# A graph network's softmax stage with attention and message columns interleaved by input feature

## The reference

```python
w_m = (efeat @ W_msg + b_msg).reshape(E, in_f, -1)
w_a = (efeat @ W_attn + b_attn).reshape(E, in_f, -1)
h_src = feat[src][:, :, None]
e1 = w_m * h_src
e2 = w_a * h_src
seg_max = jax.ops.segment_max(e2, dst, num_segments=N)
ex = jnp.exp(e2 - seg_max[dst])
denom = jax.ops.segment_sum(ex, dst, num_segments=N)
attn = ex / denom[dst]
ft = jax.ops.segment_sum(e1 * attn, dst, num_segments=N)
return ft.sum(axis=1)
```

## Time and profile before

| what | value |
|---|---|
| median of three runs | 9786.86 us |
| span of the profiled execution | 9780.2 us (the fastest of the three runs took 9780.59 us) |
| softmax loop | from 3036 to 6483 us of the span |
| one block in the loop | 20.7 us on average |
| DVE operations in the loop | 39 per block, 165 blocks |
| granted TensorE clock in the loop | 1.00 |
| other layers (conv1, conv2, rel, nn) | the rest, 6330 us |

### The profile page before, as it was taken

How to read it: one execution, slowest core, us unless ns; L and a number is a source line. 1 busy time by engine, 2 the same in 40 slices (tenths; PEclk the granted TensorE clock), 3 DMA queues, 4 the chain that set the end, 5 groups by cost and what they waited for, 6 DMA issues and landing times.

```text
span 9780.2 us, 134112 instructions
## 1 busy us (share of the span) xinstructions
PE 7946.4 (81%) x37269; PEld 4276.1 (44%) x37269; DVE 7357.8 (75%) x13651; ACT 3060.5 (31%) x12664; POOL 7256.3 (74%) x5177
## 2 busy tenths in 40 slices
PE   0899996999984777777777777745999995899994
PEld 0466663555541333333333333323655554555552
DVE  2566663454545999999999999987888885688884
ACT  0111111000004777777777777742000000000000
POOL 5677775777767777777777777745888887688887
PEclk6999996999997999999999999977999997899997
DMA  1333332222213777777777777766222221333331
GB/s 32 101 101 106 104 101 52 67 60 68 68 46 91 202 201 200 202 205 201 200 201 203 203 202 200 201 186 190 70 82 69 82 69 47 99 106 99 99 104 48
DMA packets 490722, 1215.28 MB, mean 124 GB/s; under 512 B 236141, under 2 KB 273304, under 8 KB 469836
## 3 DMA queue, kind: packets, MB, share of 16 engines
q1 hardware_dynamic: 242522, 996.22, 31.8%
q0 software_dynamic: 212624, 110.62, 9.1%
q10 hardware_dynamic: 35440, 106.85, 3.3%
HBM read 419.84 MB, written 787.23 MB: 123 GB/s over the span
## 4 chain that ended last, share of the span: by engine, by line
PE 27%; POOL 26%; issue 23%; DVE 19%; DMA 2%; DVEq 1%; SPq 1%; ACT 0%; POOLq 0%; ACTq 0%
POOL arena L559 26%; PE PS L949 21%; DVE arena L1687 5%; DVE arena L1691 4%; PE PS L971 4%; DVE arena L1733 3%; DVE arena L1700 2%; DVE arena L1711 2%; PE PS L932 1%; DVEq L1679 1%; DVE arena L1813 1%; DMA arena<-d_lane 0%; DVE tmp L1815 0%; DVE arena L1422 0%; DVE arena L1721 0%
## 5 line engine op out<-in xcount | busy, mean ns | idle before, releaser
L949 PE MATMUL PS<-arena,TB 125*128 125x500 bf16 (+1 forms) x18711 | 4067.9, 373 | 109.2 <-DVE arena L1390 109.1
L559 POOL DMA_INDIRECT arena<-d_feat,srci x1650 | 2578.1, 1562 | 842.0 <-issue 454.2
L949 PEld LDWEIGHTS PS<-arena,TB 125*128 125x128 bf16 x18711 | 1832.9, 99 | 2013.2 <-issue 174.7
L559 POOL DMA_INDIRECT arena<-d_h,srci x1485 | 1887.5, 1271 | 653.0 <-issue 433.1
L770 ACT ACTIVATE arena<-PS,arena 125x32 f32<-125x32 f32 x10560 | 2012.4, 446 | 302.8 <-PE PS L1068 263.0
L1390 DVE TENSOR_SCALAR arena<-arena,lane 125x2000 bf16<-125x2000 f16 (+2 forms) x1848 | 1228.9, 723 | 348.0 <-PE PS L949 221.9
L1402 DVE SCALAR_TENSOR_TENSOR arena<-arena,lane,PS 128x500 f32<-128x500 f16 x891 | 637.1, 715 | 1120.9 <-PE PS L949 858.5
L559 POOL DMA_INDIRECT arena<-d_rel,irel x858 | 1210.2, 1411 | 307.2 <-issue 261.2
L559 POOL DMA_INDIRECT arena<-d_nn,srci x759 | 1068.6, 1408 | 283.4 <-issue 230.4
L1115 PE MATMUL PS<-arena,ident 125*125 125x512 f32 x1650 | 873.6, 610 | 403.6 <-ACT arena L813 210.1
L1733 DVE SCALAR_TENSOR_TENSOR arena<-arena 125x512 f32<-125x512 f32 x1155 | 859.7, 744 | 20.3
(11 more groups left out here) (274 smaller groups left out, 7172.5 us busy)
## 6 DMA issues: line engine op xcount, KB each, us to landing
d_soft_max<-arena SPq DMA_DIRECT2D x165, 1120.0 KB
d_soft_den<-arena SPq DMA_DIRECT2D x330, 560.0 KB
d_soft_num<-arena SPq DMA_DIRECT2D x330, 560.0 KB
arena<-d_pick SPq DMA_DIRECT2D x66, 843.8 KB
arena<-d_lane SPq DMA_DIRECT2D x66, 843.8 KB
d_x<-arena ACTq DMA_DIRECT2D x165, 241.7 KB
arena<-d_x SPq DMA_DIRECT2D x165, 241.7 KB
d_rel<-arena SPq DMA_DIRECT2D x50, 669.4 KB
```

The costliest lines, as they stand in the source:

```text
L559: gp.indirect_dma_start(out=dst, out_offset=None, in_=table, in_offset=bass.IndirectOffsetOnAxis(ap=index, axis=0)).then_inc(S(sem), 16)
L949: ins = pe.matmul(PS[:, acc_at(L, q):acc_at(L, q) + w], TB[:, part, g * LANES * F:(g + 1) * LANES * F], OH[L][i][:, g, at:at + w], start=g ...
```

## The change

The 512 columns of `W6` are put in another order: for each input feature i, 16 attention columns and then 16 message columns. So everything behind it is interleaved as well: `XS` is parted into `XM` (maxima, 256 numbers per edge) and `XD` (pairs, 512 per edge, i x (attention, message) x 16), and a helper `paired(rows, a)` picks the attention (a = 0) or the message (a = 1) runs of 16 numbers.

With pairs interleaved, one `product` covers a whole group of two edges: 1024 elements, three per block where there were six. ACT's `scaled` reads and writes 32 numbers in one run. `weigh` now works on 2, 4 and 4 edges (three operations, 512, 1024 and 1024 elements, called w0, W2, W6) instead of five times 2. The maxima of n0 to n9, the exponentials, the first subtraction matmul and `weigh` now read or write runs of 16 numbers, 32 apart. The two sum tables become `low` and `high`, the first and the last 256 numbers of a pair row: in each, a piece of a store is 1024 bytes where it was 5120, five times as many pieces for the same bytes. Behind the loop the last row is copied apart by three new operations before the transposes, and the divisions read the interleaved layout.

```diff
-        XS = ar(o, 3 * B1 * ROW).rearrange("p (s a t c) -> p s a t c", s=3, a=3, t=B1); o += 3 * B1 * ROW
+        XM = ar(o, 3 * B1 * CH).rearrange("p (s t c) -> p s t c", s=3, t=B1); o += 3 * B1 * CH
+        XD = ar(o, 3 * B1 * 2 * CH).rearrange("p (s t c) -> p s t c", s=3, t=B1); o += 3 * B1 * 2 * CH
...
+        def paired(rows, a):
+
+            if len(rows.shape) == 3:
+                rows = rows.rearrange("p t c -> p (t c)")
+            return rows.rearrange("p (x a o) -> p x a o", a=2, o=F)[:, :, a, :]
...
+            def put_sums(b, s, t, n):
+                for a, table in enumerate(d_sums):
+                    wide_dma(sp, edges_w(table)[:, bass.ds(b * (B1 * CH) + t * CH, n * CH)].rearrange("p (t c) -> p t c", t=n),
+                             XD[:, s, t:t + n, a * CH:(a + 1) * CH], f"soft_s{s}")
...
+                wide_dma(sp, edges_w(d_smax)[:, bass.ds(b * (B1 * CH), B1 * CH)],
+                         XM[:, s].rearrange("p t c -> p (t c)"), f"soft_s{s}")
                 sp.wait_ge(S("soft_row"), b + 1)
-                put(b, s, 1, 0, B1 // 2)
-                put(b, s, 2, 0, B1 // 2)
+                put_sums(b, s, 0, B1 // 2)
                 sp.wait_ge(S("soft_done"), done)
-                put(b, s, 1, B1 // 2, B1 // 2)
-                put(b, s, 2, B1 // 2, B1 // 2)
+                put_sums(b, s, B1 // 2, B1 // 2)
...
-                bank = PS[0:P, (4 + n % 2) * 512:(5 + n % 2) * 512].rearrange("p (a i o) -> p i a o", a=2, i=F)
+                        act.wait_ge(S("soft_num"), 3 * (b - 2))
+                bank = (4 + n % 2) * 512
                 for i in range(F):
-                    ins = act.activation(PB[:, s, n].rearrange("p a (i o) -> p i a o", i=F)[:, i], bank[:, i], ACT.Copy,
-                                         scale=GH[:, s, t, i:i + 1])
+                    ins = act.activation(PB[:, s, n, 2 * F * i:2 * F * (i + 1)], PS[0:P, bank + 2 * F * i:bank + 2 * F * (i + 1)],
+                                         ACT.Copy, scale=GH[:, s, t, i:i + 1])
...
-                        act.activation(XS[:, s, 1, t:t + 2, :], bank.rearrange("p (t c) -> p t c", t=2), ACT.Exp)\
+                        act.activation(paired(XD[:, s, t:t + 2, :], 0), bank.rearrange("p (x o) -> p x o", o=F), ACT.Exp)\
...
-                        logits = XS[:, s, 1, t:t + 2, :] if t < AT else PB[:, s, t - AT:t - AT + 2, 0, :]
-                        pe.matmul(bank, ident[0:P, 0:P], logits, start=True, stop=False)
-                        pe.matmul(bank, neg, XS[:, s, 0, t:t + 2, :], start=False, stop=True).then_inc(S("soft_diff"), 1)
+                        pairs = XD[:, s, t:t + 2, :] if t < AT else PB[:, s, t - AT:t - AT + 2, :]
+                        pe.matmul(bank.rearrange("p (x o) -> p x o", o=F), ident[0:P, 0:P], paired(pairs, 0), start=True, stop=False)
+                        pe.matmul(bank, neg, XM[:, s, t:t + 2, :].rearrange("p t c -> p (t c)"), start=False, stop=True)\
+                            .then_inc(S("soft_diff"), 1)
...
-                        dve.wait_ge(S("soft_at"), NG3 * b + n // 2 + 1)
+                        dve.wait_ge(S("soft_prod"), NG3 * b + n // 2 + 1)
...
-                        logits = XS[:, s, 1, n, :] if n < AT else PB[:, s, n - AT, 0, :]
-                        prev = XS[:, s, 0, n - 1, :] if n else XS[:, (s + 2) % 3, 0, B1 - 1, :]
-                        v.scalar_tensor_tensor(XS[:, s, 0, n, :], prev, KR[:, s, n, 0:1], logits,
+                        logits = paired(XD[:, s, n, :] if n < AT else PB[:, s, n - AT, :], 0)
+                        prev = XM[:, s, n - 1, :] if n else XM[:, (s + 2) % 3, B1 - 1, :]
+                        v.scalar_tensor_tensor(wide_row(XM[:, s, n, :]), wide_row(prev), KR[:, s, n, 0:1], logits,
                                                ALU.add, ALU.max).then_inc(S("soft_max"), 1)
...
-            def product(b, s, g, a):
+            def product(b, s, g):
 
                 n, t, at = GROUPS[g], 2 * g, 2 * (g % 2) * 512
-                if a == 0:
-                    dve.wait_ge(S("soft_mm"), NG3 * b + g + 1)
-                v.tensor_tensor(XS[:, s, 1 + a, t:t + n, :].rearrange("p t (i o) -> p t i o", i=F),
-                                PS[0:P, at:at + n * 512].rearrange("p (t a i o) -> p t a i o", a=2, i=F, o=F)[:, :, a],
-                                GH[:, s, t:t + n, :].unsqueeze(3).broadcast_to([P, n, F, F]),
-                                ALU.mult).then_inc(S("soft_prod" if a else "soft_at"), 1)
+                dve.wait_ge(S("soft_mm"), NG3 * b + g + 1)
+                v.tensor_tensor(XD[:, s, t:t + n, :].rearrange("p t (i c) -> p (t i) c", i=F),
+                                PS[0:P, at:at + n * 512].rearrange("p (x c) -> p x c", c=2 * F),
+                                bc(GH[:, s, t:t + n, :].rearrange("p t i -> p (t i)"), 2 * F),
+                                ALU.mult).then_inc(S("soft_prod"), 1)
...
-                def weigh(t):
+                def weigh(t, n):
 
                     dve.wait_ge(S("soft_exp"), 6 * b + (B1 - t) // 2)
-                    rows = XS[:, s, 2, t:t + 2, :] if t < AT else PB[:, s, t - AT:t - AT + 2, 1, :]
-                    v.tensor_tensor(XS[:, s, 2, t:t + 2, :], rows,
-                                    XS[:, s, 1, t:t + 2, :], ALU.mult).then_inc(S("soft_num"), 1)
-
-                weigh(0)
+                    rows = XD[:, s, t:t + n, :] if t < AT else PB[:, s, t - AT:t - AT + n, :]
+                    sums = XD[:, s, t:t + n, :]
+                    v.tensor_tensor(paired(sums, 1), paired(rows, 1), paired(sums, 0), ALU.mult).then_inc(S("soft_num"), 1)
+
+                weigh(0, 2)
...
-                        if t % 2 == 0:
-                            dve.wait_ge(S("soft_num"), 5 * b + t // 2 + 1)
+                        if t in (2, AT):
+                            dve.wait_ge(S("soft_num"), 3 * b + (2 if t == 2 else 3))
...
-                    if t % 2:
-                        weigh(t + 1)
+                    if t == 1:
+                        weigh(2, AT - 2)
+                        yield
+                    if t == 3:
+                        weigh(AT, NA)
...
-                product(b, s, 0, 0)
-                product(b, s, 0, 1)
+                product(b, s, 0)
                 next(new)
-                product(b, s, 1, 0)
+                product(b, s, 1)
                 next(new)
-                product(b, s, 1, 1)
                 next(new)
-                product(b, s, 2, 0)
+                product(b, s, 2)
                 next(new)
                 next(new)
                 for _ in range(2):
                     next(new)
                     next(old, None)
                 next(new)
-                product(b, s, 2, 1)
...
+            dve.wait_ge(S("soft_done"), NB1)
+            v.tensor_copy(CB[:, 0:CH], XM[:, 2, B1 - 1, :])
+            v.tensor_copy(wide_row(CB[:, CH:2 * CH]), paired(XD[:, 2, B1 - 1, :], 0))
+            v.tensor_copy(wide_row(CB[:, 2 * CH:ROW]), paired(XD[:, 2, B1 - 1, :], 1)).then_inc(S("soft_tail"), 1)
...
-                link(v.tensor_scalar(rows[:, :, 0:CH], rows[:, :, CH:2 * CH], 1e-30, None, ALU.max))
+                ratio = rows[:, :, 0:CH].rearrange("p j (i o) -> p j i o", o=F)
+                pair = rows[:, :, CH:ROW].rearrange("p j (i a o) -> p j i a o", i=F, a=2)
+                link(v.tensor_scalar(ratio, pair[:, :, :, 0, :], 1e-30, None, ALU.max))
```

90 lines of the change are left out of this document (45 added, 45 removed).

## The result

Measured beside the kernel before, the kernel after took 9815.31 us (median of 20 runs, 9766.48 to 9829.00; before 9787.3 us): ratio 1.0027, 95% interval 1.0020 to 1.0033, some 26 us slower. 9777 us had been forecast. The unchanged kernel was measured twice more later, on two different chips and each time beside the kernel before: 9776.61 us (ratio 0.9987, 0.9978 to 0.9996) and 9760.89 us (ratio 0.998, 0.9971 to 0.9989). So its time is not one number (single executions of the first measurement lie between 9766 and 9829 us too), and the median of the kernel before, at 9783 to 9788 us in every measurement, has no such spread. What follows first is the execution profiled with the first measurement: span 9805.0 us, own time 9807.12.

A forecast was written before the change was run, and what follows sets the result against it. VectorE was taken to bound the softmax loop. Terms of -13 (VectorE), +0.4 (last store) and +2.5 us (behind the loop) gave -10 us, from a 9786.86 us median to 9777; own range 9760 to 9797, wide range 9733 to 9860.

The forecast's parts named there:

- What bounds the kernel: Softmax loop: VectorE's 39 instruction starts set the 20.75 us block; removed starts count unless something else comes to the front.
- the sum on VectorE: VectorE per block: 0.33 and 0.21 us saved, 0.46 lost to new dependent neighbours; -0.08 us, -13 us over 165 blocks.
- New access patterns at nothing: Runs of 16 numbers, 32 apart, on VectorE, TensorE and ScalarE: taken to cost 0 us.
- The rival of an extra step per run of 16: VectorE's n0 to n9 and w pay about 1 ns per run: 0.32 us per block, +53 us, about 9830 us; chance 0.09.
- the two rivals of a larger gain: VectorE: stalls stay hidden, about 9737 us, chance 0.15; or each removed start returns its whole fixed part, 9663 us, chance 0.02.
- TensorE ahead of t1: TensorE's L1078, which t1 waits for, ends at 9.12 us, t1 comes at 9.45: 0.3 us ahead, no cost.
- the flags: Next block's flags, behind the sums' stores in SP's queue, keep about 1.7 to 2.9 us of room: covered, 0 us.
- the stores: Sums in 1024-byte pieces take a tenth longer, about 0.5 us per second half; nothing waits for them, 0 us.
- The rival of late flags: SP's queue: slower small-piece stores delay the flags, VectorE waits 0.5 us per block, about 9860 us; chance 0.14.
- What lies beside VectorE: Other engines in the block: GpSimd's gathers start earlier, run three blocks ahead and are covered; TensorE stays ahead; 0 us.
- Behind the loop: After the softmax loop: copies covered by a gather wait, strided division reads 0 to +5 us, taken as +2.5.
- the last store: Final store of sums, in the chain with 4.10 us, gets a tenth longer: +0.4 us.

The follow-up runs named there:

- the run with big pieces in six issues: Kernel after, with sums stored in pieces of 10,240 bytes instead of 1024 and six store issues per block instead of ten: 9769.44 us (ratio 0.9983).

## Why the prediction was wrong, point by point

- *What bounds the kernel* held while no gather was late, and *the sum on VectorE* held in its parts. Forecast -0.08 us per block with -0.03 to -0.13 as the same reading; measured 20.75 to 20.61, -0.14, just outside. Its parts: p0 to n0 4848.44 - 4847.18 = 1.26 (1.25 forecast), p1 to the next start 1.13 (1.133), n1 to n2 1.00 - 0.48 = 0.52, n7, n8 and n9 0.60 and 0.61 apart (0.60). The 0.06 us beyond the sum are two places that it left out. Averaged over the steady blocks, from t8 to the first product it takes 0.71 us before and 0.66 after, and from n6 to c 0.42 before and 0.40 after, together 0.07. The first stood in the earlier trace rows: 4851.93 - 4851.15 = 0.78, where a sum takes 0.66; one block of three has it, the two others have 0.67.
- *New access patterns at nothing* held: the products last 1.22 us, n0 to n9 482 ns against 478. The rival of an extra step per run of 16 is out, and so are the two rivals of a larger gain: the new neighbours do stall, and two starts that become one give back 2 x 0.60 - 1.13 = 0.07 us, not 0.15. The section "The DRAIN you can't avoid" of the page "VectorE: DVE Perf Modes" in the Trainium skill, on which the second of these rested, also says that a next operation that is not held starts earlier. The rows agree with that: the next start is 0.60 us behind one that lasts 0.68.
- *TensorE ahead of t1*, *the flags* and *the stores*: covered, as forecast; the DMA share went to 0.74 as forecast. The rival of late flags did not come.
- *What lies beside VectorE* is the step that failed: "GpSimd's gathers, which wait for them, start earlier and run three blocks ahead, so they are covered." I took a gather's duration as given. It hangs on VectorE's order: with W2 and W6 merged, one gather of a block is held for 5 us, the same gathers went from 1562 to 1764 ns, GpSimd's 2.3 us of room per block went, and the first user of a gather is not VectorE but ScalarE, with 15 us of slack and not three blocks. Priced from the profiled executions, the step is +41 us in the first measurement, +12 in the second (two long blocks) and 0 in the third, where the sum had 0.
- *Behind the loop* and the last store: L1832 lasts 1011 ns against 992, together +0.2 us where I took +2.5. It does not matter.
- No rival had this mechanism. In the first measurement the kernel got slower where a small gain had been forecast, and the time came out above the forecast's own range (9760 to 9797), inside the wide one. The 9777 us of the second measurement is the forecast to the microsecond, by luck: VectorE gave back 23 us and not 13, and two long blocks took 12. The 9761 us of the third is at the lower end of the own range, since nothing took the larger gain away. Neither makes the step right: the 5-us gather is there in all three, and GpSimd waits for VectorE's products at most 0.6 us per block, where it waited 2.3.

## What to carry to other kernels

Merging operations on a full VectorE saved 0.07 us per start here, but the place of each operation is also a place where other engines get on: look at the durations on GpSimd before and after, not at its instructions alone. In these runs no gather took over 2.9 us where the sums had a product that reads PSUM, or the end of a product, every 3 us or so. With p0 moved into the sums the same 34 operations run at 9739 us, and merging only the numerator products in the old layout does as well. The slack of a transfer is the time to its first user on any queue. A queue whose work fills the whole period keeps every delay: here the slack fell by a step at each held gather and came back only when a hold was missed. Before believing a difference of 0.5% in such a case, measure it on a second chip.

## What the runs showed of the hardware that I had not expected

- A gather of 1.21 us on GpSimd took 4.99 us in the middle of the sums and 16.26 us beside 32 independent scalar-tensor-tensor operations with two SBUF tensors, and ended 1.09 us behind the last of them. VectorE's own operations were not longer for it (0.66 us apart, 21.29 us for 32).
- The way out was the end of a product of two SBUF tensors (1.08 and 1.09 us before the gather's end) or the start of a product that reads PSUM (1.16 us).
- The same program ran at 9761, 9777 and 9815 us on three occasions, in medians of 11 to 20 runs, while the kernel before stayed at 9783 to 9788 us.
- Gathers and VectorE's block kept step: in the run with big pieces in six issues the slack stood at 6.4 us for 57 blocks running, and in all runs with VectorE's order of the kernel after it mostly changed in steps.
- A store of 125 rows in one issue left half the DMA engines' time unused and cost some 1150 us against two issues of 112 and 13 rows.
